# A selective-scan block on one core: the state input of 12 of 32 states moved from VectorE to GpSimd

## The reference, cut to what matters

```python
def step(h, inputs):
    dt_t, x_t, B_t, C_t = inputs
    h = h * jnp.exp(dt_t[..., None] * A) + (dt_t * x_t)[..., None] * B_t[:, None, :]
    y = jnp.einsum('bds,bs->bd', h, C_t)
    return (h, y)
```

## Time and profile of the kernel before

| what | value |
|---|---|
| median of 3 runs | 16819.14 us (16817.72 to 16821.2) |
| the profiled execution's own time | 16829.66 us |
| its span, first to last instruction | 16827.8 us |
| mean granted TensorE clock | 0.928 of full speed |
| DVE busy | 16304.7 us, 97% of the span |
| PE busy | 12705.6 us, 76% |
| POOL busy | 11262.8 us, 67% |
| ACT busy | 8208.2 us, 49% |
| DMA | mean 81 GB/s; the one hardware queue's packets took 26.0% of 16 engines' span |

### The profile page before, as it was taken

The page is one execution under the profiler, slowest core; times in us unless marked ns, Lnnn a source line. Parts: engine busy times, 40 slices in busy tenths (PEclk is TensorE's granted clock), DMA queues, the critical chain, the costliest instruction groups (busy, mean ns, idle before and its releaser), DMA issues.

```text
span 16827.8 us, 151142 instructions
## 1 busy us (share of the span) xinstructions
PE 12705.6 (76%) x27588; PEld 4838.1 (29%) x27588; DVE 16304.7 (97%) x14970; ACT 8208.2 (49%) x14979; POOL 11262.8 (67%) x4884
## 2 busy tenths in 40 slices
PE   4777777777777777777777777777777777777776
PEld 1222222222222222222222222222222222222222
DVE  6999999999999999999999999999999999999997
ACT  3454544544454454444544445454454445544453
POOL 4766666666666666667666666666666666666664
PEclk7999999999999999999999999999999999999998
DMA  3232222322223222232222322222232222322222
GB/s 82 74 93 72 78 88 74 93 73 76 89 74 90 74 78 88 73 91 74 80 86 74 90 75 88 77 79 87 73 93 74 76 88 74 92 73 78 87 75 72
DMA packets 765005, 1356.81 MB, mean 81 GB/s; under 512 B 345916, under 2 KB 494852, under 8 KB 761636
## 3 DMA queue, kind: packets, MB, share of 16 engines
q1 hardware_dynamic: 763908, 1345.60, 26.0%
HBM read 1190.26 MB, written 115.67 MB: 78 GB/s over the span
## 4 chain that ended last, share of the span: by engine, by line
DVE 41%; issue 37%; PE 9%; ACT 5%; POOL 3%; DVEq 2%; SPq 1%; DMA 1%; ACTq 0%; POOLq 0%
DVE u_in L1029 19%; DVE h L1041 17%; PE y_ps L807 4%; POOL hc L565 2%; SPq L391 1%; PE proj_ps L766 1%; ACT a_ps L664 1%; PE b_ps L855 1%; DVE xc L1057 1%; DVEq L1039 1%; DMA x<-x_dram 1%; DVEq L1027 1%; PE proj_ps L788 1%; PE side_ps L818 1%; DVE stats L899 1%
## 5 line engine op out<-in xcount | busy, mean ns | idle before, releaser
L565 POOL TENSOR_TENSOR hc<-h,c_sb 128x1024 f32<-128x1024 f32 x4096 | 10315.5, 2518 | 5143.7 <-DVE h L1041 4760.5
L664 ACT ACTIVATE a_ps<-dt,a_neg 128x512 f32<-128x512 f32 x8192 | 5648.8, 691 | 8281.9 <-DVE h L1041 8271.7
L1041 DVE TENSOR_TENSOR_SCAN h<-a_ps,carry,u_in 128x512 f32<-128x512 f32 x7168 | 8928.2, 1269 | 39.6 <-ACT carry L670 20.0
L807 PE MATMUL y_ps<-hc,ident 128*128 128x512 f32 x16396 | 8492.9, 643 | 200.8 <-DVE xc L1057 177.3
L1029 DVE TENSOR_TENSOR u_in<-dtx,b_ps 128x1024 f32<-128x1024 f32 x4096 | 4898.6, 1196 | 137.7 <-PE b_ps L855 103.6
L807 PEld LDWEIGHTS y_ps<-hc,ident 128*128 128x128 f32 x16396 | 3265.7, 204 | 3224.7 <-issue 2647.6
L855 PE MATMUL b_ps<-b_parts,select 96*128 96x512 bf16 x4096 | 1669.8, 408 | 2114.6 <-DVE u_in L1029 2053.0
L855 PEld LDWEIGHTS b_ps<-b_parts,select 96*128 96x128 bf16 x4096 | 412.4, 101 | 4609.0 <-DVE u_in L1029 4033.4
L766 PE MATMUL proj_ps<-u_ln,w_x 128*128 128x512 f32 x2064 | 1135.7, 634 | 475.2 <-ACT u_ln L616 258.3
L1041 DVE TENSOR_TENSOR_SCAN h<-a_ps,u_in 128x512 f32<-128x512 f32 x1024 | 1225.4, 1208 | 13.5 <-DVE halo L956 4.6
L818 PE MATMUL side_ps<-padded,w_main 128*128 128x512 f32 x1632 | 894.5, 635 | 26.2 <-DVE padded L940 9.5
(11 more groups left out here) (97 smaller groups left out, 5653.9 us busy)
## 6 DMA issues: line engine op xcount, KB each, us to landing
c_sb<-c_dram SPq DMA_DIRECT2D x2052, 512.0 KB, 3.7
raw<-x SPq DMA_DIRECT2D x17, 2048.0 KB
x_dram<-vmax SPq DMA_DIRECT2D x68, 512.0 KB, 5.3
x<-x_dram SPq DMA_DIRECT2D x136, 256.0 KB, 8.5
z<-x_dram SPq DMA_DIRECT2D x68, 512.0 KB, 7.8
out<-raw SPq DMA_DIRECT2D x272, 128.0 KB
x_dram<-x SPq DMA_DIRECT2D x129, 256.0 KB, 4.4
edge<-padded SPq DMA_DIRECT2D x1632, 16.0 KB
```

Source lines behind the costliest of these rows:

```text
L565: pool.tensor_tensor(hc[:, s % RING], h[:, s % RING], c_sb[:, s // C_GROUP % C_RING, s % C_GROUP:s % C_GROUP + 1, :].broadcast_to([P, NH, T]),
L664: act.activation(a_ps[:, a_slot(c * S + s, half)], dt[:, c % 2, half], ACT.Exp, scale=a_neg[:, at:at + 1]).then_inc(a_made, 1)
L807: mm = pe.matmul(y_ps[:, half], ident[:, :], hc[:, s % RING, half], start=(s == 0), stop=(s == S - 1), skip_group_check=True)
L1041: dve.tensor_tensor_scan(h[:, r, half], a_ps[:, a_slot(c * S + s, half)], u_in[:, r, half], start, ALU.mult, ALU.add).then_inc(h_done, 1)
```

## The change

For 12 of the 32 states of each chunk (`POOL_U`: 1, 4, 6, 9, 11, 14, 16, 19, 21, 26, 28, 31) `u_in` is made by GpSimd, right after the `hc` of four states earlier. Its second operand is no longer `b_ps`: the row of B is stored to DRAM in float32 together with the rows of C, and a DMA from SP spreads it over 128 partitions into a new tile `b_sb` with two buffers. `u_in` gets four buffers instead of two. PE no longer makes `b_ps` for those 12 states, and the selecting table keeps 20 blocks. The loads of C rows carry one state instead of two, still with four buffers. The diff, cut to its core:

```diff
-C_GROUP, C_RING = 2, 4
+C_GROUP, C_RING = 1, 4
+U_RING = 4
+B_RING = 2
+POOL_U = [s for s in range(S) if (13 * s + 20) % S < 12]
+DVE_U = [s for s in range(S) if s not in POOL_U]
...
-                sp.dma_start(c_dram[(c + 1) % 2], c_rows[S:2 * S, :]).then_inc(c_stored, 16)
+                sp.dma_start(bc_dram[(c + 1) % 2], bc_rows[0:2 * S, :]).then_inc(c_stored, 16)
...
+            def load_b(b, j):
+                if j >= B_RING:
+                    sp.wait_ge(pu_made, made_by_pool(b, j - B_RING))
+                row = POOL_U[j % NP]
+                sp.dma_start(b_sb[:, j % B_RING, :],
+                             bc_dram[j // NP % 2, row:row + 1, :].partition_broadcast(P)).then_inc(b_in[j % B_RING], 16)
...
                         if s % C_GROUP == C_GROUP - 1:
                             load_c(b, c, s // C_GROUP + C_RING)
+                        if (s + U_RING) % S in POOL_U:
+                            load_b(b, pool_index(*behind(c, s, -U_RING)) + B_RING)
...
+            def make_u(b, c, s):
+                j = pool_index(c, s)
+                if s == POOL_U[0]:
+                    pool.wait_ge(dtx_done, chunk(b, c, NH))
+                pool.wait_ge(b_in[j % B_RING], b_loads(b, j))
+                if c or s >= U_RING:
+                    pool.wait_ge(h_done, state(b, *behind(c, s, U_RING), NH))
+                pool.tensor_tensor(u_in[:, s % U_RING], dtx[:, c % 2],
+                                   b_sb[:, j % B_RING:j % B_RING + 1, :].broadcast_to([P, NH, T]),
+                                   ALU.mult).then_inc(pu_made, 1)
...
+                        if (s + U_RING) % S in POOL_U:
+                            make_u(b, *behind(c, s, -U_RING))
...
-            act.activation(select[:, :], x1[0:3 * S, :], ACT.Copy).then_inc(setup_a, 1)
+            for k, s in enumerate(DVE_U):
+                made = act.activation(select[:, k * P:(k + 1) * P], x1[0:3 * S, s * P:(s + 1) * P], ACT.Copy)
+            made.then_inc(setup_a, 1)
...
-                act.activation(c_rows[S:2 * S, :], proj_ps[S:2 * S, :], ACT.Copy)
+                act.activation(bc_rows[0:2 * S, :], proj_ps[0:2 * S, :], ACT.Copy)
...
-                        pe.wait_ge(u_made, state(b, *behind(c, s, 1)))
-                        pe.matmul(b_ps[:, :], sel, b_parts[:, c % 2, :], start=True, stop=True).then_inc(b_cast, 1)
+                        if s in DVE_U:
+                            k = DVE_U.index(s)
+                            pe.wait_ge(u_made, made_by_vector(b, c, s) - 1)
+                            pe.matmul(b_ps[:, :], select[:, k * P:(k + 1) * P], b_parts[:, c % 2, :],
+                                      start=True, stop=True).then_inc(b_cast, 1)
...
-                    dve.wait_ge(u_made, state(b, c, s))
+                    if s in DVE_U:
+                        dve.wait_ge(u_made, made_by_vector(b, c, s))
+                    else:
+                        dve.wait_ge(pu_made, made_by_pool(b, pool_index(c, s)))
...
-                        if s + 1 < S or c + 1 < NC:
+                        if (s + 1 < S or c + 1 < NC) and (s + 1) % S in DVE_U:
                             make_u(b, *behind(c, s, -1))
```

More of the change, by code:

```diff
@@ L57 @@
 AHEAD = 4
-C_GROUP, C_RING = 2, 4
+C_GROUP, C_RING = 1, 4
 A_RING = 3
+U_RING = 4
+B_RING = 2
+POOL_U = [s for s in range(S) if (13 * s + 20) % S < 12]
+DVE_U = [s for s in range(S) if s not in POOL_U]
+ND, NP = len(DVE_U), len(POOL_U)
+U_AHEAD = sum(s < U_RING for s in POOL_U)
 LAG = 3
@@ L136, in build @@
     x2_dram = nc.dram_tensor("x2_dram", (TH, P, TW), F32, kind="Internal").ap()
-    c_dram = nc.dram_tensor("c_dram", (2, S, T), F32, kind="Internal").ap()
+    bc_dram = nc.dram_tensor("bc_dram", (2, 2 * S, T), F32, kind="Internal").ap()
     with ExitStack() as ctx:
@@ L154, in build @@
         halo_keep = sb("halo_keep", [P, 4])
-        select = sb("select", [3 * S, S * P], BF16)
+        select = sb("select", [3 * S, ND * P], BF16)
         w_x = sb("w_x", [P, TAPS, DI])
@@ L203, in build @@
         parts = sb("parts", [S, 3, T], BF16)
-        c_rows = dt_rows = cen
+        bc_rows = dt_rows = cen
         b_parts = sb("b_parts", [3 * S, 2, T], BF16)
-        u_in = sb("u_in", [P, RING, NH, T])
+        u_in = sb("u_in", [P, U_RING, NH, T])
+        b_sb = sb("b_sb", [P, B_RING, T])
         h = sb("h", [P, RING, NH, T])
@@ L258, in build @@
         c_in = [sem(f"c_group_in{r}") for r in range(C_RING)]
-        u_made = sem("state_input")
+        u_made = sem("state_input_by_vector")
+        pu_made = sem("state_input_by_pool")
+        b_in = [sem(f"b_row_in{r}") for r in range(B_RING)]
         a_made = sem("decay")
@@ L303, in start_ahead, with made_by_vector, made_by_pool, pool_index @@
                 engine.sem_inc(semaphore, AHEAD * n)
+        def made_by_vector(b, c, s):
+            return (b * NC + c) * ND + DVE_U.index(s) + 1 + AHEAD
+        def made_by_pool(b, j):
+            return b * (NC * NP) + j + 1 + AHEAD
+        def pool_index(c, s):
+            return c * NP + POOL_U.index(s)
+        def b_loads(b, j):
+            return (b * (NC * NP) + j) // B_RING * 16 + 16
         def kept_state(b, c, s):
@@ L410, in load_c @@
                     sp.wait_ge(hc_done, state(b, c, (k - C_RING) * C_GROUP + C_GROUP - 1))
-                rows = c_dram[(c + k // GROUPS) % 2, k % GROUPS * C_GROUP:(k % GROUPS + 1) * C_GROUP, :]
+                first = S + k % GROUPS * C_GROUP
+                rows = bc_dram[(c + k // GROUPS) % 2, first:first + C_GROUP, :]
                 sp.dma_start(c_sb[:, k % C_RING], rows.partition_broadcast(P)).then_inc(c_in[k % C_RING], 16)
+            def load_b(b, j):
[4 more added lines that the diff above has]
+                             bc_dram[j // NP % 2, row:row + 1, :].partition_broadcast(P)).then_inc(b_in[j % B_RING], 16)
             def store_x2(b, use):
@@ L467, in _ @@
                 load_c(0, 0, k)
+            for j in range(B_RING + U_AHEAD):
+                load_b(0, j)
             sp.sem_inc(stored, BAND * 16)
@@ L511, in _ @@
                 sp.wait_ge(c_in[r], c_loads(B, 0, r))
+            for j in range(U_AHEAD, U_AHEAD + B_RING):
+                sp.wait_ge(b_in[j % B_RING], b_loads(B, j))
         @block.gpsimd
@@ L555, in _ @@
                 dt_times_x(0, -1, half)
-            start_ahead(pool, hc_done)
+            start_ahead(pool, hc_done, pu_made)
+            for s in range(U_RING):
+                if s in POOL_U:
+                    make_u(0, 0, s)
             with pool.Fori(0, B) as b:
@@ L852, in _ @@
                     for s in range(S):
-                        sel = select[:, s * P:(s + 1) * P]
-                        pe.wait_ge(u_made, state(b, *behind(c, s, 1)))
-                        pe.matmul(b_ps[:, :], sel, b_parts[:, c % 2, :], start=True, stop=True).then_inc(b_cast, 1)
+                        if s in DVE_U:
[3 more added lines that the diff above has]
+                                      start=True, stop=True).then_inc(b_cast, 1)
                         sum_states(b, *behind(c, s, LAG))
@@ L1024, in make_u @@
             def make_u(b, c, s):
-                if s == 0:
+                if s == DVE_U[0]:
                     dve.wait_ge(dtx_done, chunk(b, c, NH))
-                dve.wait_ge(b_cast, state(b, c, s))
-                dve.wait_ge(h_done, state(b, *behind(c, s, RING), NH))
-                dve.tensor_tensor(u_in[:, s % RING], dtx[:, c % 2],
+                dve.wait_ge(b_cast, made_by_vector(b, c, s))
+                if c or s >= U_RING:
+                    dve.wait_ge(h_done, state(b, *behind(c, s, U_RING), NH))
+                dve.tensor_tensor(u_in[:, s % U_RING], dtx[:, c % 2],
                                   b_ps[:, :].unsqueeze(1).broadcast_to([P, NH, T]), ALU.mult).then_inc(u_made, 1)
@@ L1037, in scan @@
                         dve.wait_ge(kept, kept_state(b, *behind(c, s, RING)))
-                    dve.wait_ge(u_made, state(b, c, s))
+                    if s in DVE_U:
+                        dve.wait_ge(u_made, made_by_vector(b, c, s))
+                    else:
+                        dve.wait_ge(pu_made, made_by_pool(b, pool_index(c, s)))
                 dve.wait_ge(a_made, state(b, c, s, NH) - (NH - 1 - half))
                 start = carry[:, half, s:s + 1] if c else 0.0
-                dve.tensor_tensor_scan(h[:, r, half], a_ps[:, a_slot(c * S + s, half)], u_in[:, r, half], start,
+                dve.tensor_tensor_scan(h[:, r, half], a_ps[:, a_slot(c * S + s, half)], u_in[:, s % U_RING, half], start,
                                        ALU.mult, ALU.add).then_inc(h_done, 1)
@@ L1100, in _ @@
             with dve.Fori(0, B) as b:
-                make_u(b, 0, 0)
+                if 0 in DVE_U:
+                    make_u(b, 0, 0)
                 for c in range(NC):
```

## The result

The changed kernel takes 17619.53 us (median of 4 runs, 17597.15 to 17635.23) against 16820.17 us: 1.0474 times the time before, interval 1.0456 to 1.0493. It is slower by 799 us, where the forecast was some 220 us faster and its range ended at 16,920 us. The profiled execution has a span of 17633.4 us.

The account below looks back on a forecast made before the run. VectorE was taken to set the pace nearly everywhere. Per image -46 + 21 + 8 + 3 = -14 us, times 16 is -224, with the start -219, giving 16,600 us; range 16,080 to 16,920.

Parts of the forecast that it names:

- What leaves VectorE: On VectorE, 1536 products go, each giving back its step of 1.12 us, 1720 us in all.
- What GpSimd gets: On GpSimd, each new product priced like a plain `hc`, 2.31 us start to start; floor 14,290 us before any wait.
- The walk: Plain states stepped through by rules with two buffers between VectorE and GpSimd: gain 46 us per image, ends 20 and 108.
- the sum: Terms added per image: -46 + 21 + 8 + 3 = -14 us; times 16 is -224, with the start -219.
- Two-input products against GpSimd: VectorE products of two SBUF tensors and GpSimd instructions exclude each other: 21 us per image lost, ends 0 and 84.
- C and B rows: C rows queued on SP behind x1 loads and output stores land late, B rows covered: 8 us per image, ends 0 and 25.
- TensorE: In-order TensorE loses 96 products per image, but waits for its sums hurt more: 3 us per image, ends -5 and 25.
- C, slower by the locks: Rival: GpSimd is mid-step whenever VectorE brings a two-input product, 48 per image; about 17,180 us, mild form 16,900; chance 0.18.
- The signs: Expected in the changed profile: POOL busy above 90%, 2560 `u_in` on VectorE, `hc` waits some 50 us per image.
- the sign of D: Rival of no tellable change, 16,820 us, chance 0.08; its sign: POOL waits for `c_sb` DMA over 10 us per image.

## Why the prediction was wrong

**What leaves VectorE**: right. 2560 products are left at an unchanged 1198 ns.

**What GpSimd gets**: right within 4%; the plain product takes 2.31 us from start to start in the timeline above, and its mean of 2396 ns has the exclusion in it.

**The walk**: of 107.5 us removed per image it let 46 arrive, so VectorE was to wait 61.5 for `hc`, 984 us in all. 756 us were measured, some of it for late C rows (155 us in the kernel before with that edit alone), and four buffers of h gave 328 to 355 us back. The waits are of the kind that it forecast, and its size was high. What the sum put at nothing were VectorE's waits for ACT: for its first split they rose from 78 to 209 us, for `a_ps` from 5 to 123. That the removed products had covered these latencies before is my reading; no run shows it.

**Two-input products against GpSimd: this step failed.** I put it at 21 us per image, 336 us in all, where VectorE's instructions grew by 1,090 us, 68 per image. It had two grounds, and both were wrong. The list held only products with two SBUF inputs; g1, a tensor_scalar, was missing, and taking it off VectorE gave 324 us. And "half is absorbed by the engine that is ahead" does not hold: taking the split off VectorE gave 371 us, more than its lengthening of 213 and its own 84 together. The two kinds give 695 us; less the 152 us that they took before the change, 543 are left, 34 per image, before dilation and column products are counted. For the gate the runs do not decide. The step also took one wait to end with the running GpSimd instruction, and g1 and the column products waited through three.

**C and B rows**: the term was 8 us per image, 128 us; the edit alone cost 130 in the kernel before. That is close in part by luck: almost a third of the waits stand behind the load of raw, which the term had only in its upper end. No wait for a row of B appears.

**TensorE**: 3 us per image was too little: VectorE's and GpSimd's waits for it rose by 160 and 40 us, 12 per image. The granted clock fell from 0.928 to 0.907 and the mean product of `y_ps` rose from 643 to 670 ns; no run separates the clock from the rest.

**The rivals**: C, slower by the locks, was the case that came, given 0.18; it set 35 us per image as the point where the change turns slower. Its place was only partly right, as it left out g1. g1 (324 us), split (371) and four buffers (328 to 355) are shown by runs. These overlap, and part of each is no loss by the change, as the same three edits give 153 us in the kernel before; I can't split the 799 us into a sum of causes.

**A balance of VectorE's time**, per image, which says where time went and not why: 107.5 us removed; added 68 of lengthening, 47 of waiting for `hc`, 19 for ACT, 10 for TensorE and 4 for the rest. The last 11 are lost overlap. Neighbouring instructions on VectorE overlap by 1167 us in all before and 888 after. 110 us of that went with the moved products (1536 x 0.076), and the other 169 fit the waits: 1989 gaps of over 0.1 us where there were 562. Together this makes an image about 51 us slower, and 50 were measured (799 / 16). The forecast was 14 us faster, and the locks are the largest part of the difference.

**The signs**: `u_in` on VectorE 2560 times, 47 us of waiting for `hc` per image and a mean `hc` of 2.49 us came as said. GpSimd was busy for 83%, not for over 90. And the sign of D came as well: GpSimd waited for C rows for 216 us, 13.5 per image where 10 was the mark.

## What to carry to other kernels

Before work is given to GpSimd, list every VectorE instruction that can't run beside it: those with two SBUF inputs, however short, and those tensor_scalars from SBUF to SBUF whose trace shows it (here 512 and 1536 elements did, 1280 and a single column did not). Their present price says little, because an idle GpSimd hides it; what counts is how GpSimd stands at their place once it is busy. Move these few first (here 130 + 129 instructions were worth 695 us, 152 of it their own length), then give the two engines more buffers between them, and only then judge the move itself.

## What the runs showed of the hardware that I had not expected

- VectorE can be passed over by GpSimd instructions that follow each other without a gap. 63 of 130 tensor_scalars of g1 (0.52 us free) took 5.7 us, and 15 of 36 two-input products on one column (0.16 us free) took 5.3, through one partial and two whole ones. The gate waited for the running one only (2.64 us in the example, at most 3.40).
- Beside a GpSimd memset, two-input products run free (1202 ns) and the tensor_scalar of g1 does not (1990 ns).
- A tensor_scalar of five rows of 256 elements ran beside GpSimd without loss on either side (1.57 us); one of six rows took 1.56 us instead of 1.06 and held `hc` up to 3.07.
- A GpSimd product of one tensor with itself and bf16 output took 1895 ns for 1024 elements, where two different float32 inputs with float32 output take 2350.
